# The first mixture of experts: products with the experts' weights ahead of the gates, their gelu kept in place, and the router's logits with the router's weights at rest

## The reference

```python
logits = xf @ gate_w.T                      # 625 x 8 experts
probs = jax.nn.softmax(logits, axis=-1)
top_w, top_i = jax.lax.top_k(probs, K)      # K = 2
top_w = top_w / (jnp.sum(top_w, axis=-1, keepdims=True) + 1e-09)
...
hidden = jax.nn.gelu(jnp.einsum('ecd,edh->ech', padded, w1) + b1[:, None, :], approximate=False)
out = jnp.einsum('ech,ehd->ecd', hidden, w2) + b2[:, None, :]
expert_out = out[se, pos] * pw[:, None]
final = jnp.zeros((T, D), x.dtype).at[pt].add(expert_out)
```

## Time and profile before

| | |
|---|---|
| time, median of 3 runs (range) | 2146.84 us (2140.87 to 2151.06) |
| the profiled execution: its time / its span | 2146.55 us / 2144.5 us |
| TensorE busy with matmuls | 1901.9 us, 89% of the span |
| VectorE, ScalarE, GpSimd busy | 1348.9, 904.6, 221.8 us |
| mean granted TensorE clock | 0.94 of full |

### The profile page before, as it was taken

How to read it: one execution, slowest core, us unless ns; L and a number is a source line. 1 busy time by engine, 2 the same in 40 slices (tenths; PEclk the granted TensorE clock), 3 DMA queues, 4 the chain that set the end, 5 groups by cost and what they waited for, 6 DMA issues and landing times.

```text
span 2144.5 us, 30883 instructions
## 1 busy us (share of the span) xinstructions
PE 1901.9 (89%) x12258; PEld 1806.1 (84%) x12259; DVE 1348.9 (63%) x2448; ACT 904.6 (42%) x1469; POOL 221.8 (10%) x169
## 2 busy tenths in 40 slices
PE   5978989979997985678876799999999999999998
PEld 4866879978887985567876789999999999999998
DVE  6997766343235566587777466335665656766787
ACT  2331114313131431276544422333555656666776
POOL 0000000012000000375541000000010100000110
PEclk9998998987999998789987999999999999999999
DMA  2110020100111110201002212225465656776896
GB/s 108 45 45 1 23 89 30 52 24 23 45 67 58 68 38 30 76 21 36 16 1 104 91 67 85 79 71 199 177 224 180 231 210 220 242 251 231 280 316 219
DMA packets 36795, 234.29 MB, mean 109 GB/s; under 512 B 5916, under 2 KB 7318, under 8 KB 14632
## 3 DMA queue, kind: packets, MB, share of 16 engines
q1 hardware_dynamic: 31318, 217.41, 28.4%
q0 software_dynamic: 2656, 8.99, 1.9%
q10 hardware_dynamic: 2674, 5.87, 0.7%
HBM read 221.91 MB, written 10.35 MB: 108 GB/s over the span
## 4 chain that ended last, share of the span: by engine, by line
PE 71%; DVE 15%; issue 8%; ACT 3%; DMA 2%; POOL 1%; SPq 0%; DVEq 0%; ACTq 0%; POOLq 0%
PE bank L312 15%; PE bank L314 14%; PE bank L313 14%; PE bank L2417 7%; PE bank L569 3%; PE bank L2418 3%; PE bank L2429 3%; DVE weight_lo L285 2%; PE bank L2433 2%; PE bank L2421 1%; PE bank L2430 1%; PE bank L2432 1%; DVE mix_kv L792 1%; PE bank L2420 1%; POOL gat_edge L1793 1%
## 5 line engine op out<-in xcount | busy, mean ns | idle before, releaser
L285 DVE TENSOR_TENSOR weight_lo<-weight_raw,weight_hi 128x2304 fp32r<-128x2304 f32 (+1 forms) x155 | 389.1, 2513 | 41.6 <-ACT weight_hi L275 41.4
L275 ACT ACTIVATE weight_hi<-weight_raw 128x2304 fp32r<-128x2304 f32 (+1 forms) x155 | 323.1, 2087 | 89.2 <-DMA weight_raw<-in_ffn_w 48.7
L312 PE MATMUL bank<-xT_hi,weight_hi 128*128 128x306 f32 (+1 forms) x576 | 184.3, 320 | 6.4 <-DVE mix_kv L1576 2.5
L313 PE MATMUL bank<-xT_lo,weight_hi 128*128 128x306 f32 (+1 forms) x576 | 178.9, 311 | 0.0
L314 PE MATMUL bank<-xT_hi,weight_lo 128*128 128x306 f32 (+1 forms) x576 | 178.6, 310 | 0.0
L312 PE MATMUL bank<-weight_hi,xT_hi 128*128 128x384 f32 (+1 forms) x480 | 161.5, 336 | 9.8 <-DVE xT_lo L333 4.5
L2791 DVE TENSOR_TENSOR hidden_tmp<-hidden_tmp,bank 128x160 f32<-128x160 f32 (+5 forms) x192 | 65.6, 341 | 158.6 <-ACT hidden_tmp L2577 158.6
L313 PE MATMUL bank<-weight_lo,xT_hi 128*128 128x384 f32 (+1 forms) x480 | 157.6, 328 | 0.0
L314 PE MATMUL bank<-weight_hi,xT_lo 128*128 128x384 f32 (+1 forms) x480 | 157.5, 328 | 0.0
L569 PE MATMUL bank<-one_hot_dst,one_hot_src 125*128 125x313 f16 x800 | 122.6, 305 | 15.2 <-ACT packed_counts L583 7.9
L312 PE MATMUL bank<-weight_hi,hidden_hi 128*128 128x384 f32 (+1 forms) x366 | 124.4, 340 | 0.0
(11 more groups left out here) (477 smaller groups left out, 5254.4 us busy)
## 6 DMA issues: line engine op xcount, KB each, us to landing
weight_raw<-in_ffn_w SPq DMA_DIRECT2D x111, 1152.0 KB, 5.2
weight_raw_fifth<-in_ffn_w SPq DMA_DIRECT2D x25, 1152.0 KB, 5.2
weight_raw<-in_shared_w SPq DMA_DIRECT2D x16, 1152.0 KB, 5.3
weight_raw<-in_mix_kv SPq DMA_DIRECT2D x8, 1152.0 KB, 6.2
weight_raw<-in_gat_w SPq DMA_DIRECT2D x8, 768.0 KB, 4.3
weight_raw<-in_mix_q SPq DMA_DIRECT2D x4, 1152.0 KB, 5.2
weight_raw<-in_mix_out SPq DMA_DIRECT2D x4, 1152.0 KB, 5.1
weight_raw<-in_gnn_w SPq DMA_DIRECT2D x4, 1152.0 KB, 5.1
```

The source lines that it names most:

```text
L275: act.activation(upper_, whole_, ACT.Copy).then_inc(*w_hi.one())
L285: dve.tensor_tensor(lower_, whole_, upper_.bitcast(F32), ALU.subtract).then_inc(*w_lo.one())
L312: pe.matmul(dst, a[0], b[0], start=first, stop=False)
L313: pe.matmul(dst, a[0], b[1], start=False, stop=False)
```

## The change

Logits: the router's weights are now at rest (128x8), and the tokens move, 320 wide, in two products of 18 matmuls into 8 partitions. ScalarE copies the two results, five small transposes (L1202 of the changed kernel) turn them, and one copy fills `p`.

Order: seven units (EARLY) are multiplied ahead of the gates: units 0 and 1 ahead of the logits, 2 to 5 between the logits and the edge counts, 6 behind the gates' transposes. Their gelu results wait in `ffn0_acted`, a tile of full size that lies in the memory of `ffn0_hT_lo`, so each is later multiplied, and replaced by its lower part, in place. The seven picks follow in one run. From unit 7 on product and pick alternate as before. The split of chunk c0 + 3 stands ahead of unit 6's gelu on ScalarE and ahead of the first multiplication on VectorE; it stood behind unit 5 on both. In the second half gelu waits for the sums of the first. The pads behind token 626 are no longer blanked; the last tile's sums have 114 rows in place of 128.

```diff
-        hT = pair("ffn0_hT", [P, HK, TP], scope)
-        tmp = sb("ffn0_tmp", [P, 2, 320], F32, scope)
+        hT_hi = sb("ffn0_hT_hi", [P, HK, TP], F32R, scope)
+        with ExitStack() as whole_scope:
+            acted = sb("ffn0_acted", [P, HK, TP], F32, whole_scope)
+        hT = (hT_hi, sb("ffn0_hT_lo", [P, HK, TP], F32R, scope))
+        logit_rows = sb("ffn0_logits_of_experts", [E, TP], F32, scope)
         count_f = sb("count_float", [P, TT, TP], F32, scope)
+        LOGIT_SPANS = ((0, 320), (320, 320))
+
+        ROWS = [P] * (TT - 1) + [LAST + 1]
+        EARLY = 7
...
+        def unit(i):
+            hid = i // 2
+            a0, n = SPANS[i % 2]
+            return hid, hid % HK, slice(a0, a0 + n), n
+
         def tensor():
-            logits_tensor(gp, logit_banks, xT_ready)
...
+            def logits():
+                pe.wait_ge(*gate_lo.at(1))
+                for s, (a0, n) in enumerate(LOGIT_SPANS):
+                    bank = ring.next(logits_kept.at(s + 1))
+                    logit_banks.append(bank)
+                    product(bank[0:E, 0:n], [(at(gp, ALL, k, ALL), at(xT, ALL, k, slice(a0, a0 + n))) for k in range(KD)]).then_inc(*logits_full.one())
+
+            def logits_turned():
+                pe.wait_ge(*logits_kept.at(2))
+                bank = ring.next(logits_kept.at(3))
+                logit_banks.append(bank)
+                for t in range(TT):
+                    end = pe.transpose(bank[:, t * E:(t + 1) * E], logit_rows[:, tok(t)], ident[0:E, 0:E])
+                end.then_inc(*logits_full.one())
+
+            def counts_turned():
...
+            def hidden(i):
+                hid, _, span, n = unit(i)
+                w = weight("ffn0_w1", i // 6)
+                pe.wait_ge(*xT_ready)
+                bank = ring.next(gelu.at(i + 1))
+                hid_banks.append(bank)
+                mm = hid % 3
+                product(bank[:, 0:n], [(at(w, ALL, k, slice(mm * P, (mm + 1) * P)), at(xT, ALL, k, span)) for k in range(KD)]).then_inc(*hid_full.one())
+
+            def picked(i):
+                hid, _, span, n = unit(i)
+                bank = ring.next(gated.at(i + 1))
+                pick_banks.append(bank)
+                product_exact_a(bank[:, 0:n], [(sel[:, hid, :], at(gT, ALL, span))]).then_inc(*pick_full.one())
...
+            hidden(0)
+            hidden(1)
+            logits()
+            hidden(2)
+            logits_turned()
+            hidden(3)
+            hidden(4)
+            hidden(5)
+            counts_turned()
             gates_tensor(gates, gate_banks)
+            hidden(6)
             pe.wait_ge(*gT_lo_made.at(TT))
             pe.wait_ge(*sel_made.at(1))
+            for i in range(EARLY):
+                picked(i)
             for kh in range(2):
-                for c in range(2):
...
+                for i in range(max(EARLY, 12 * kh), 12 * (kh + 1)):
+                    hidden(i)
+                    picked(i)
+                pe.wait_ge(*h_lo.at(12 * (kh + 1)))
...
         def scalar():
+            def hidden(i):
+                hid, k, span, n = unit(i)
+                act.wait_ge(*hid_full.at(i + 1))
+                if i >= 12:
+                    act.wait_ge(*y_full.at(2 * TT))
+                act.activation(acted[:, k, span], hid_banks[i][:, 0:n], ACT.Gelu, bias=b1[:, hid:hid + 1]).then_inc(*gelu.one())
+
+            def hidden_upper(i):
+                _, k, span, _ = unit(i)
+                act.wait_ge(*gated.at(i + 1))
+                upper(at(hT, ALL, k, span), acted[:, k, span]).then_inc(*h_hi.one())
+
             act.wait_ge(*gate_in.at(16))
             upper(at(gp, ALL, ALL, ALL), gate[:, :, :]).then_inc(*gate_hi.one())
-            logits_scalar(p, logit_banks)
+            act.wait_ge(*b1_in.at(16))
+            hidden(0)
+            hidden(1)
+            for s, (a0, n) in enumerate(LOGIT_SPANS):
+                act.wait_ge(*logits_full.at(s + 1))
+                act.activation(logit_rows[:, a0:a0 + n], logit_banks[s][0:E, 0:n], ACT.Copy).then_inc(*logits_kept.one())
+            hidden(2)
+            act.wait_ge(*logits_full.at(3))
+            act.activation(p[:, :, :], logit_banks[2][:, 0:TT * E].rearrange("p (t e) -> p t e", e=E), ACT.Copy).then_inc(*logits_kept.one())
             act.wait_ge(*soft_low.at(1))
             act.activation(p[:, :, :], p[:, :, :], ACT.Exp).then_inc(*soft_exp.one())
+            hidden(3)
+            act.wait_ge(*sel_filled.at(3))
+            act.activation(sel[:, :, :], sel_f[:, :, :], ACT.Copy).then_inc(*sel_made.one())
+            hidden(4)
+            act.wait_ge(*b2_in.at(16))
+            upper(at(b2p, ALL, ALL), b2[:, :]).then_inc(*b2_hi.one())
+            hidden(5)
             act.wait_ge(*count_f_made.at(TT))
             for i in range(2 * TT):
                 t, (k0, kn) = i // 2, PARTS[i % 2]
                 act.wait_ge(*count_turned.at(i + 1))
                 act.activation(count[:, t, k0 * P:(k0 + kn) * P], count_banks[i][:, 0:kn * P], ACT.Copy).then_inc(*count_kept.one())
             gates_scalar(gT, gate_banks)
-            act.wait_ge(*sel_filled.at(3))
...
+            weight_read[c0] = hid_full.at(6)
+            weights_hi(c0)
+            hidden(6)
+            for i in range(EARLY):
+                hidden_upper(i)
             for kh in range(2):
-                for c in range(2):
...
+                for i in range(max(EARLY, 12 * kh), 12 * (kh + 1)):
+                    hidden(i)
+                    hidden_upper(i)
+                    if i % 6 == 5:
+                        c = i % 12 // 6
+                        weight_read[c0 + 4 * kh + c] = hid_full.at(i + 1)
+                        weights_hi(c0 + 4 * kh + c)
...
         def vector():
+            def hidden(i):
+                _, k, span, n = unit(i)
+                dve.wait_ge(*gelu.at(i + 1))
+                dve.wait_ge(*pick_full.at(i + 1))
+                dve.tensor_tensor(acted[:, k, span], acted[:, k, span], pick_banks[i][:, 0:n], ALU.mult).then_inc(*gated.one())
+                dve.wait_ge(*gated.now())
+                dve.wait_ge(*h_hi.at(i + 1))
+                lower(at(hT, ALL, k, span), acted[:, k, span]).then_inc(*h_lo.one())
...
-            gates_vector(gT, gate_banks)
             dve.wait_ge(*b2_hi.at(1))
             lower(at(b2p, ALL, ALL), b2[:, :]).then_inc(*b2_lo.one())
-            dve.memset(tmp[:, 0, :], 0.0).then_inc(*pad_made.one())
-            dve.wait_ge(*pad_hi.at(1))
-            lower(at(hT, ALL, ALL, slice(T + 1, TP)), tmp[:, 0, 0:HK * (TP - T - 1)].rearrange("p (k n) -> p k n", k=HK)).then_inc(*h_lo.one())
+            gates_vector(gT, gate_banks)
+            weights_lo(c0)
             dve.wait_ge(*x_ready)
             for kh in range(2):
-                for c in range(2):
...
+                for i in range(12 * kh, 12 * (kh + 1)):
+                    hidden(i)
+                    if i % 6 == 5 and i > 5:
+                        weights_lo(c0 + 4 * kh + i % 12 // 6)
...
-                    for t in range(TT):
+                    for t, n in enumerate(ROWS):
                         i = 2 * TT * kh + TT * c + t
                         dve.wait_ge(*y_full.at(i + 1))
-                        dve.tensor_tensor(x[:, t, cols], x[:, t, cols], y_banks[i][:, 0:HALF], ALU.add).then_inc(*y_added.one())
+                        dve.tensor_tensor(x[0:n, t, cols], x[0:n, t, cols], y_banks[i][0:n, 0:HALF], ALU.add).then_inc(*y_added.one())
```

More of the change, by code:

```diff
@@ L1092, in router_memory @@
         return gate, gp, gT, best, number, hot, work, rest, gates
-    def logits_tensor(gp, banks, xT_ready):
-        pe.wait_ge(*gate_lo.at(1))
-        pe.wait_ge(*xT_ready)
-        for t in range(TT):
-            bank = ring.next(logits_kept.at(t + 1))
-            banks.append(bank)
-            product(bank[:, 0:E], [(at(xT, ALL, k, tok(t)), at(gp, ALL, k, ALL)) for k in range(KD)]).then_inc(*logits_full.one())
-    def logits_scalar(logits, banks):
-        for t in range(TT):
-            act.wait_ge(*logits_full.at(t + 1))
-            act.activation(logits[:, t, :], banks[t][:, 0:E], ACT.Copy).then_inc(*logits_kept.one())
     def top_two_vector(p, best, number, hot, work, rest):
```

77 lines of the change are left out of this document (16 added, 61 removed).

## The result

The changed kernel takes 2115.16 us (median of 4 runs, 2112.07 to 2118.85), the kernel before beside it 2147.31 us. The ratio is 0.9854, 95% interval 0.9825 to 0.9883: 1.5% faster. The forecast was 2122.5 with a range from 2116 to 2130, so the direction held, and the time lies 0.8 us under the range. The losses that the change was to remove are gone; what ends last ahead of the first sums, and what the other stages do, came out otherwise than forecast. The profiled execution took 2118.85 us.

What follows compares the result with a forecast made beforehand. TensorE, busy 89% of the span, bounds the kernel with five losses in this stage. First sums 25.7 us earlier, less 1.7 for the clock, is 24.0 off 2146.55: 2122.5 us, range 2116 to 2130.

Steps and rivals of the forecast that it cites:

- Unit 0 at clock 1.00: Sign at the stage's start: unit 0 about 0.1 us behind `xT_lo`, at full clock.
- logits 5.3 us: Sign at the router's logits on TensorE: 5.3 us in place of 19.2.
- gates hidden: Gates ready at 495.4 under units 3 to 5, no TensorE wait; uncovered they would cost 4.8 us.
- no bank wait over 1 us: Sign in units 7 to 11 on TensorE: a bank wait over 1 us would prove the forecast wrong; 0.2 us allowed.
- the first multiplication directly behind the split: Sign on VectorE: first multiplication directly behind the lower part of c0 + 3, some 31.5 us behind `xT_lo`.
- ScalarE's and VectorE's lane. Here the new limit forms: Ahead of the first sums: this chain ends last, at 523.4, so they start at 523.45, 25.7 us earlier.
- rival 2: Clock stays up at the first sums: 25.7 us, 2120.9; with a faster chain TensorE alone sets 521.7, 2119; chance 0.32.
- 16 us from 504.3: TensorE's own work for units 7 to 11; with 0.2 us of bank waits, picks said to end at about 519.6.
- 1.7 us for the clock at the new wait: Loss taken off for half clock behind a 3.8 us TensorE wait ahead of the first sums.
- The sum for this stage: Total gain claimed for the first mixture of experts: 25.7 - 1.7 = 24.0 us.
- Nothing in the other stages changes but when it starts: All stages outside the first mixture of experts: no gain or loss, 0 us.
- The rule on the clock: Edge counts and gates, 30 transposes on TensorE, hold full clock and add nothing to the sum.

Runs made afterwards that it cites:

- e5: Changed kernel with the split of chunk c0 + 3 moved behind unit 9 on ScalarE and VectorE; 2115.89 us, ratio 0.9869.
- e8: Changed kernel unaltered, run again for a third trace; 2113.47 us.
- e15: Changed kernel with 12 matmuls more (2 us) in front of the last sum of the first mixture of experts; 2117.8 us, one execution.
- e16: Changed kernel with 18 matmuls more (3 us) in front of the last sum of the first mixture of experts; 2124.16 us, one execution.
- shifted kernels: Kernel before with 1 or 2 us of extra matmuls, changed kernel with 2 or 3 us, before the stage's last sum; 2144.83, 2147.83, 2117.8, 2124.16 us.
- e9: e4 with units 7, 8 and 9 put between the seven picks; 2117.47 us, ratio 0.9879.
- e2: Kernel before with only the new logits (router's weights at rest); 2130.58 us, ratio 0.9942.
- e3: Changed kernel with the old logits (90 matmuls of 8 columns, tokens at rest), so the new order only; 2126.74 us, ratio 0.9912.
- e4: Changed kernel whose first sums of tiles 0 and 1 wait only for unit 10 (22 in the second half), not the last; 2109.72 us, ratio 0.9835.

## Why the prediction was right and where it was wrong

**Right.** Unit 0 at clock 1.00 (472.46), logits 5.3 us (477.71 to 483.0), gates hidden, no bank wait over 1 us, the first multiplication directly behind the split. The first sums came 82.86 - 56.56 = 26.3 us earlier in the pair of traces that the prediction compares, and 27.0 in the means of four; it said 25.7. By what follows it is luck that the two are so close.

**The step "ScalarE's and VectorE's lane. Here the new limit forms" failed.** With first multiplications at 503.45 and the pace that VectorE kept, the twelve units would be done at about 521.5, half a us ahead of the 522.01 measured; the last gelu waits 0.38 us for TensorE's product at 519.86. TensorE ends last, as in the second half of rival 2, and the time of TensorE's picks is the same in e5, where VectorE had 2.5 us more. The margin is small: TensorE had lost about 1.7 us to the half clock behind its picks, and without that the chain would have ended last, as forecast, but about 1 us sooner than it said. Three sizes were off: a unit was about 1.5 us and stayed so with gelu on ScalarE (I counted 1.53 and 1.58, but gelu of the next unit runs during VectorE's lower part of this one); a pick in a row was 0.31 us and not 0.48; and the clock fell behind the picks, which cost TensorE about 1.7 us (clock 0.52 for 2.4 us and 0.73 for 2.0). A sum was wrong too: 16 us from 504.3, and 0.2 us for banks, end at 520.5 and not at 519.6, so its own numbers gave a wait of 2.9 us and not 3.8, and TensorE alone in rival 2 would have given 522.6 and not 521.7. The wait was 1.71 us.

**The term "1.7 us for the clock at the new wait" was about right for a wrong reason.** The forecast drew a line between pauses of 2 us (full clock) and 4 us (half). There is none: behind 1.71 us the clock fell at both sums in three traces of six, 1.5 us each, and at neither in e8, e15 and e16. On average it costs 1.5 us; in the four unaltered traces 2.2.

**The sum for this stage** was 24.0; the pair shows 207.75 - 184.35 = 23.4, and the means of four 208.84 - 183.65 = 25.2.

**The step that missed the time is "Nothing in the other stages changes but when it starts".** It put the other stages at nothing. That is true of the work and not of the time. In the means of four the attention takes 0.7 us less, gat 3.6 less, and the rest 1.3 more, together 3.0. The shifted kernels show gat at 283.7 in the kernel before and at 289.9 us in the changed one, by where the clock happens to fall. That the changed kernel starts gat at a favourable place is, as far as the runs show, luck and no merit of the change. I had put nothing for it; the range had 3 us of spread below rival 2's best, for the runs of one kernel, and none for a shift of the stages behind.

The miss of 7.3 us adds up so: 1.6 since 2146.55, one execution, stood for a kernel whose 29 runs average 2144.9; 1.2 in the stage; 3.0 in the other stages; 2.1 since the traces are 28.2 us apart and all runs 30.3, mostly because the traced executions of the changed kernel were slower than its others; less 0.6 between its median 2115.16 and the mean of its 11 runs, 2114.6. The two kernels' traces scatter by up to 4 us in a stage, so the 1.2 and the 3.0 are means of four and no more exact than that.

**The rule on the clock** held. The windows from 494.0 to 500.2 stay at 1.00 through 30 transposes and the unit behind them, and in e9 the clock stays up to 508: edge counts and gates didn't lower it. The layer norm's transposes say more, since TensorE stands still for 8.40 us ahead of them and does nothing else until they end. In the changed kernel they start at 465.45:

```profile
466.00:468.50 2.50, 2.50 (x14) 2.50 (x13) 2.50 (x5) 1.69 (x4) 0.00 (x0) 0.50 0.00 0
468.60:470.40 1.80, 1.80 (x17) 1.58 (x15) 1.80 (x5) 1.75 (x6) 0.00 (x0) 1.00 0.05 9
```

The clock rises while they run, in all 18 traces. By the rule of the Trainium skill ("TensorE: Matmul & The Clock Gate", Part 4: PE-mode transpose), the full clock doesn't engage for transposes, so it should have stayed at 0.50 there; these traces disagree.

What stays open: why a pause of 1.1 to 1.7 us is followed by half clock in one execution and not in another. In the traces it goes with where the clock fell or rose earlier, both at the sums and in gat. That is read from 12 traces, four of each kernel and four shifted ones, each shift run once; what sets the place of the earlier fall was not tried.

## What to carry to other kernels

Where an engine waits for a chain that its own earlier work feeds, put independent products ahead of the chain and let their results wait in place. Here each part alone left the other's loss in place: 5.6 us of waiting for the gates with the fast logits (e2), the slow logits with the new order (e3).

Before you take a trace's time as the kernel's, count the pauses of 1 to 4 us in it: each may or may not bring some 3 us of half clock, worth about 1.5 us, and one stage of this kernel took 283.5 to 289.9 us with the same instructions. A forecast by parts needs that spread in its range, on the stages that are not changed as well.

Taking away a short pause can pay more than its length: without the two pauses of 1.71 us the stage was 3.6 us shorter than the changed kernel's one trace without half clock behind them, and 6.6 us shorter than the three with it (e4).

## What the runs showed of the hardware

- The clock fell without a pause in a row of matmuls with 8 moving columns and 128x128 at rest (e3, half from 480.6 on), and behind seven picks over 8 rows (right behind 502.4 in the changed kernel; not in the one trace of e9, where they are spread).
- The clock rose from 0.50 to 1.00 while TensorE did nothing but transposes (changed kernel, 466.0 to 470.4).
- A pause of 1.11 us was followed by 0.50 (e16) and one of 1.19 us by 1.00 (changed kernel), at the same place in the program.
- Three loads of ScalarE's table of functions took 1.28 us each in the changed kernel (at 475.42, 486.47 and 488.01), and the next instruction of ScalarE started at most 0.02 us behind each. No wait of TensorE followed from them.
